# Two-layer deformable and whitening convolution: pieces of one channel half by 2048 pixels in the second pass, and twelve sixteenths of image 0 held in SBUF between its statistics and its convolution

## What is computed

```
x = x + deform_conv(group_norm(x))    # layer 0: statistics of every image, a convolution that gives
                                      # values v and sampling offsets, bilinear sampling of v, 1x1 out
x = x + zca_whiten(group_norm(x))     # layer 1: one 16-channel covariance over ALL images, its inverse
                                      # square root, then a 256x256 (block-diagonal) map of every pixel
```

## Time and profile before

| | us |
|---|---|
| median of 3 executions | 6123.9 |
| lowest, highest | 6122.75, 6130.23 |
| the profiled execution's own time | 6122.9 |
| its span in the trace | 6121.2 |
| busy VectorE, TensorE (matmul), GpSimd | 4902.5 (80%), 4252.8 (69%), 3889.7 (64%) |
| DRAM read, written | 1074.6 MB, 536.9 MB |

### The profile page before, as it was taken

How to read it: one execution, slowest core, us unless ns; L and a number is a source line. 1 busy time by engine, 2 the same in 40 slices (tenths; PEclk the granted TensorE clock), 3 DMA queues, 4 the chain that set the end, 5 groups by cost and what they waited for, 6 DMA issues and landing times.

```text
span 6121.2 us, 66619 instructions
## 1 busy us (share of the span) xinstructions
PE 4252.8 (69%) x16382; PEld 2641.4 (43%) x16382; DVE 4902.5 (80%) x12991; ACT 960.4 (16%) x2076; POOL 3889.7 (64%) x4115
## 2 busy tenths in 40 slices
PE   4867777777677767776777677767777554459776
PEld 2434444444444444444444444444444333344322
DVE  7888888888898889887988898888888666557554
ACT  1211111111111111111111111111111111100000
POOL 0077777777777777777777777777777777730000
PEclk9989988999899989888989899899888677779999
DMA  8978777888787878777887788877777554459999
GB/s 281 309 250 269 258 258 253 267 270 264 239 278 260 266 250 275 261 256 242 284 266 262 244 269 269 267 254 233 235 235 235 160 174 152 153 198 394 421 421 409
DMA packets 931609, 1612.85 MB, mean 263 GB/s; under 512 B 80944, under 2 KB 605872, under 8 KB 929456
## 3 DMA queue, kind: packets, MB, share of 16 engines
q0 software_dynamic: 196608, 537.13, 26.5%
q10 hardware_dynamic: 595968, 536.90, 25.8%
q1 hardware_dynamic: 138928, 537.74, 25.7%
HBM read 1074.58 MB, written 536.87 MB: 263 GB/s over the span
## 4 chain that ended last, share of the span: by engine, by line
POOL 59%; issue 21%; ACTq 6%; DVE 5%; DMA 4%; PE 3%; POOLq 0%; DVEq 0%; ACT 0%; SPq 0%
POOL patch L923 59%; ACTq L1314 6%; DMA out_dram<-patch 1%; DMA xs_mem<-x_dram 1%; DVE bst L438 1%; DVE patch L622 1%; DVE vring L505 1%; DMA v<-vring 1%; DMA patch<-x 0%; PE psA L1031 0%; DMA patch<-x_dram 0%; PE psO L1173 0%; PE psT L1173 0%; PE psA L1173 0%; DMA patch<-v,index_now 0%
## 5 line engine op out<-in xcount | busy, mean ns | idle before, releaser
L923 POOL DMA_INDIRECT patch<-v,index_now x4096 | 3883.8, 948 | 1530.7 <-issue 1528.8
L1031 PE MATMUL psA<-wB,xa_mem 128*128 128x364 f32 x3824 | 1525.4, 545 | 728.3 <-DVE taps L517 720.2
L622 DVE TENSOR_TENSOR patch<-patch,psI 128x384 f32<-128x384 f32 x2048 | 1038.0, 548 | 546.9 <-DMA patch<-v,index_now 516.4
L1031 PEld LDWEIGHTS psA<-wB,xa_mem 128*128 128x128 f32 x3824 | 787.1, 218 | 1339.7 <-DVE taps L517 919.4
L1063 PE MATMUL psO<-sampT,wO_sb 128*128 128x512 f32 x2048 | 973.5, 620 | 0.0
L1091 PE MATMUL psG<-x1T 128*128 128x129 f32 x4096 | 615.0, 313 | 434.3 <-DVE gram L658 433.4
L1091 PEld LDWEIGHTS psG<-x1T 128*128 128x128 f32 x4096 | 576.6, 225 | 461.7 <-issue 238.0
L1197 ACT ACTIVATE vring<-vring 128x512 f32<-128x512 f32 x512 | 320.2, 625 | 2413.9 <-DVE vring L505 2413.9
L1077 PE MATMUL psT<-ident,xr_mem 128*128 128x128 f32 x2048 | 312.5, 302 | 389.0 <-DVE xr_mem L649 388.4
L1063 PEld LDWEIGHTS psO<-sampT,wO_sb 128*128 128x128 f32 x2048 | 392.4, 202 | 400.2 <-issue 399.9
L1077 PEld LDWEIGHTS psT<-ident,xr_mem 128*128 128x128 f32 x2048 | 264.5, 158 | 506.3 <-issue 420.3
(11 more groups left out here) (213 smaller groups left out, 2941.0 us busy)
## 6 DMA issues: line engine op xcount, KB each, us to landing
v<-vring ACTq DMA_DIRECT2D x128, 2048.0 KB, 13.4
xa_mem<-x_dram SPq DMA_DIRECT2D x128, 1024.0 KB, 9.6
xr_mem<-x_dram SPq DMA_DIRECT2D x128, 1024.0 KB, 6.4
x<-xr_mem ACTq DMA_DIRECT2D x128, 1024.0 KB
xs_mem<-x_dram SPq DMA_DIRECT2D x112, 1024.0 KB, 6.6
patch<-v,index_now POOLq DMA_INDIRECT x4096, 3.8
patch<-x SPq DMA_DIRECT2D x64, 1024.0 KB, 14.2
out_dram<-patch ACTq DMA_DIRECT2D x64, 1024.0 KB, 32.5
```

Source lines behind the costliest of these rows:

```text
L622: eng.tensor_tensor(two, two, w4[:, 2 * v:2 * v + 2, 0:3].unsqueeze(3).to_broadcast([P, 2, 3, CG]), ALU.mult)
L923: eng.indirect_dma_start(out=patch[n][:, t, :], out_offset=None, in_=v2_flat[k], in_offset=bass.IndirectOffsetOnAxis(ap=index_now[n][:, t: ...
L1031: mm = eng.matmul(conv_bank[wide][r][:, 0:NA], xa[m][j][:, c, r * W:(r + 1) * W], wB[:, c, :], start=(c == 0), stop=(c == CC - 1))
```

## The change

It has three pieces.

**Second pass.** A piece is now one channel half by 2048 pixels: the same 1 MB, now 128 rows of 8 KB. Pieces 0 to 7 of an image are the lower half, 8 to 15 the upper. The number of pieces, matmuls, additions, loads and stores is unchanged.

**Statistics of image 0.** All 16 pair tiles have their own place in SBUF: pairs 12 to 15 ("passing", loaded and measured first) lie in the two `xa_mem`, `xs_mem` and `samp_mem`; pairs 0 to 7 in the four `patch` buffers (2 MB transfers); pairs 8 and 9 in `xr_mem`, pairs 10 and 11 in the two `xa_mem`, after the passing tiles there have been measured. Only those last two, and image 1's first tile in `xs_mem`, wait for VectorE.

**Convolution of image 0.** Pairs 0 to 11 (`HELD` = 12) are read by TensorE where they lie. Twelve loads of 1 MB go; pairs 12 to 15 are loaded again as before. For this first call SyncE's and TensorE's 16 pairs are written out instead of looped.

```diff
+HELD = 12
+AGAIN = tuple(range(HELD, PAIRS))
+YB = 4 * BP
+NY = CC * PIX // YB
...
+        held = [two[:, :, k * (2 * BP):(k + 1) * (2 * BP)] for two in held_two for k in range(2)]
+        held += [mem[:, :, :, :].rearrange("p c j n -> p c (j n)") for mem in (*xr_mem, *xa_mem)]
+        passing = [mem[:, :, :, :].rearrange("p c j n -> p c (j n)") for mem in (*xa_mem, xs_mem)]
...
+        y_half = [j // (PIX // YB) for j in range(NY)]
+        y_at = [j % (PIX // YB) * YB for j in range(NY)]
...
             def load_s(b, i):
+                if isinstance(b, int) and isinstance(i, int) and (b, i) == (1, 0):
+                    eng.wait_ge(st0_used, len(AGAIN))
...
             def load_a(b, i, m):
+                if stays(b, i):
+                    return
...
-                    with eng.Fori(0, PIX // S0 // 2) as i:
-                        for j in range(2):
-                            at = eng.snap((i * 2 + j) * S0)
-                            eng.wait_ge(st0_used[j], i + 1)
-                            alone(eng)
-                            eng.dma_start(xs0[j], x_v[s, :, :, bass.ds(at, S0)])\
-                               .then_inc(st0_ld[j], 16)
+                    for i in AGAIN:
+                        eng.dma_start(passing[i - HELD], x_v[s, :, :, i * (2 * BP):(i + 1) * (2 * BP)])\
+                           .then_inc(piece_ld[i], 16)
+                    for n in range(RING):
+                        eng.dma_start(held_two[n], x_v[s, :, :, n * (4 * BP):(n + 1) * (4 * BP)])\
+                           .then_inc(piece_ld[2 * n], 16)
+                    for i in range(2 * RING, HELD):
+                        if i >= HELD - 2:
+                            eng.wait_ge(st0_used, i - (HELD - 2) + 1)
+                            alone(eng)
+                        eng.dma_start(held[i], x_v[s, :, :, i * (2 * BP):(i + 1) * (2 * BP)])\
+                           .then_inc(piece_ld[i], 16)
...
-                eng.dma_start(y_buf[j], x1_v[0, :, :, j * YB:(j + 1) * YB]).then_inc(y_ld[j], 16)
+                eng.dma_start(y_buf[j], x1_v[0, :, y_half[j], y_at[j]:y_at[j] + YB]).then_inc(piece_ld[j], 16)
...
+                        row = held[i][:, c, (j * ROWS + r) * W:(j * ROWS + r + 1) * W] if stays(b, i) \
+                            else xa[m][j][:, c, r * W:(r + 1) * W]
```

More of the change, by code:

```diff
@@ L194, in deform_zca_kernel @@
         map_v = sem("map_v")
-        y_ld = [sem(f"y_ld{j}") for j in range(NY)]
+        piece_ld = [sem(f"piece_ld{j}") for j in range(NY)]
         y_mm = sem("y_mm")
@@ L226, in run, with pairs @@
             image(B - 2, B - 1, None, None)
-        def pairs(eng, pair):
+        def pairs(eng, pair, unrolled=False):
+            if unrolled:
+                for i in range(PAIRS):
+                    pair(i, i % 2, i // 2)
+                return
             for i in range(2):
@@ L309, in deform_zca_kernel @@
         cnow = area(biasB, CC * P, CC)
-        y_buf = [mem[:, :, :, :].rearrange("p c j n -> p c (j n)") for mem in (*xa_mem, xs_mem)]
+        y_buf = [mem[:, :, :, :].rearrange("p c j n -> p (c j n)") for mem in (*xa_mem, xs_mem)]
         y_buf += [v[:, half * ROWS:(half + 1) * ROWS, :, :, :].rearrange("p r g k e -> p (r g k e)")
[L312 to L315, removed]
+                  for v in vring for half in range(2)]
+        y_buf += [weight[:, :]]
+        y_buf += [area(p_n[:, :, :].rearrange("p j e -> p (j e)"), k * YB, YB)
+                  for p_n in patch for k in range(2)]
+        y_half = [j // (PIX // YB) for j in range(NY)]
+        y_at = [j % (PIX // YB) * YB for j in range(NY)]
         y_bank = ((*psO, *psA), (*psT, psI, psG))
@@ L391, in pair @@
                         load_r(g, i, m, q)
-                pairs(eng, pair)
+                pairs(eng, pair, g is None)
             def first_conv():
@@ L729, in image @@
                 if a is None and g is None:
[L730 to L737, removed]
-                                                       xs0[j][:, c, n * BP:(n + 1) * BP])
-                            ins.then_inc(st0_used[j], 1)
+                    for i in (*AGAIN, *range(HELD)):
+                        src = held[i] if i < HELD else passing[i - HELD]
+                        if not (i < 2 * RING and i % 2):
+                            eng.wait_ge(piece_ld[i], 16)
+                        for c in range(CC):
+                            for n in range(2):
+                                ins = eng.bn_stats(bst[:, c, i * 2 + n, :], src[:, c, n * BP:(n + 1) * BP])
+                        ins.then_inc(st0_used, 1)
                     return
@@ L1020, in conv_rows @@
             def conv_rows(b, i, m, q, j, rows, wide):
-                if j == 0 and 0 in rows:
-                    eng.wait_ge(xa_ld[m], (b * (PAIRS // 2) + q) * 16 + 16)
+                if j == 0 and 0 in rows and not stays(b, i):
+                    eng.wait_ge(xa_ld[m], xa_turn(b, q))
                 for r in rows:
```

51 lines of the change are left out of this document (26 added, 25 removed).

## The result

| | kernel before | changed kernel |
|---|---|---|
| median of 9 executions each, us | 6125.36 | 6110.16 |
| lowest, highest | 6121.14, 6130.43 | 6103.56, 6111.59 |
| ratio to before, 95% interval | | 0.9971 [0.9962, 0.9979] |
| the profiled execution's own time, span | 6122.9, 6121.2 | 6105.31, 6103.6 |
| DRAM read, MB | 1074.6 | 1062.0 |

The account below looks back on a forecast made before the run. The fetch block was taken as fixed, the second pass as bound by DMA bytes over rate, and the front as improvable. Gains of 9.9 + 2.3 + 8.8 + 1.0 + 12.5 = 34.5 us took 6122.9 to 6088.4 us, range 6072 to 6105.

Parts of the forecast that it names:

- the prediction's own sign: Reasons count as wrong if the front gains under 15 or over 28 us, or the second pass runs at ≤422 or 436 GB/s.
- 1. Statistics: Statistics of image 0, start to `prep`: loads end the stage at 51.4 us instead of 61.28, -9.9 us.
- 2. First period: Up to pair 2's first eviction: image 1's second statistics tile lands in 7.0 us instead of 9.28, -2.3 us.
- 3. The 13 pairs: Convolution of image 0: DMA stops binding, each pair falls from 12.76 to 12.08 us, VectorE's chain; -8.8 us.
- 4. The last v store: Image 0's last v store, before the first fetch: lands sooner than 14.86 us behind a shorter backlog, -1.0 us.
- 5. Second pass: Second pass: 8 KB rows raise the DMA rate from 421 to 430 GB/s, 597.8 to 585.3 us, -12.5 us.
- A: Rival: second pass stays at 421 GB/s, only the front gains, 22.0 us; 6101 us in all, chance 0.14.
- B: Rival: second pass reaches the ceiling of 437 GB/s, -21.9 us beside the front's -22.0; 6079 us, chance 0.12.
- E: Rival: second-pass stores in 8 KB rows lose rate, +53 us against the front's -22; 6154 us, chance 0.03.
- Rival C: Second pass gets half the gain, 425 GB/s, -5.7 us in that term; 6095 us, chance 0.16.
- rival D: Pairs stay at 12.76 us, last v store no sooner; only statistics, first period and half the second-pass gain: 6105 us, chance 0.05.

Follow-up runs that it names:

- half_pass: The changed kernel with its second pass ended after 4 of 8 images, the other four outputs left out; executed once, span 6922.5 us.
- rows_only: The kernel before with only the second pass changed to the new pieces with 8 KB rows; 7262.34 us, 0.9993 of the kernel before.
- v_first: The changed kernel with SyncE's loads after image 1's last statistics tile held until image 0's last v store landed; 6108.38 us, 0.9957 of the kernel before.
- after_again: The changed kernel unaltered, measured again on another chip; 7332.26 us, 0.9975 of the kernel before.

## Why the prediction was wrong

The direction and the separation into front and second pass held. Of the five places named, three gained less than forecast (the statistics, the 13 pairs, the second pass) and two gained nothing. By the prediction's own sign its reasons for the front were wrong: the first fetch came 10.5 us earlier, where less than 15 was to count as that and 22.0 was forecast.

*1. Statistics, -9.9 against -6.8.* The step that failed is the path. The sum let the loads end the stage ("Last byte at 48.5 us, 0.3 us to its wait, four `bn_stats`"), with VectorE alone 0.8 us shorter ("VectorE alone would need 50.5 us"). The last byte came near its forecast, at 49.0 us, but VectorE was 3.0 us behind it. Its own chain was the longer one: the first `bn_stats` at 12.06 us instead of 11.5, 64 of them at 0.61 us, and two stops, 2.49 us for the first 2 MB transfer and 0.68 us later, together 54.3 us of the 54.46. I had counted the landing of a double tile's bytes and not that nothing of it may be used before its end. With single tiles the stage is 1.15 us shorter and the loads are its bound again. (The "16 tiles in 9.78 us" of the prediction are 16 `bn_stats`, which is four pair tiles.)

*2. First period, -2.3 against +0.7.* The second statistics tile landed in 8.82 us, not 7.0. The step that failed is "it shares the engines with the first v store and with the load of pair 2's `xa_mem`. That load goes". In both kernels the tile moves no byte for the first 4.0 us, in which the v store, issued 4.4 us ahead of it, is all but finished; the load of `xa_mem` was issued behind the tile, and taking it away brought 0.46 us. Whether the tile's packets stood behind the store's in the engines or were formed late, the runs don't tell. One more thing stands in this stretch: the first eight matmuls of the convolution, 2.77 us in the chain before, take 3.93.

```profile
69.65 2.77 PE psA L1031 x8
```
```profile
62.81 3.93 PE psA L1058 x8
```

This 1.16 us is the difference of two executions and isn't shown to be the change's. In TensorE's timelines the same eight take 2.8 to 4.3 us in the 14 profiles of kernels whose TensorE pairs are written out (4.1 in the changed kernel, 2.8 in half_pass), and 3.0 and 3.2 us in before and rows_only. I had set written-out code at nothing, with about 1 us a pair as its worst case, for which I had no row; no later pair shows any such cost.

*3. The 13 pairs, -8.8 against -5.0.* The DMA did stop binding (share 0.86 to 0.90), and VectorE's chain did come next, as the forecast said. What failed is "I read 12.08 us as VectorE's own chain for a pair". The shortest pair of a loop of two is the one without the branch; the mean of both, 12.21, is the floor: 13 x 0.13 = 1.7 us. The rows had said so: VectorE's waits for transfers summed to 6.9 us, and the 1.9 us missing to 8.8 were called near. The other 2.2 us are the ends of the stage, by VectorE's first taps eviction of each pair: the first pair takes 13.1 us, the last two 12.7 and 12.8. "absorbed by two `vring` buffers" was wrong for the statistics tile, which has one buffer (two waits on the chain, for the tiles issued at 225.7 and 238.8 us; a third, for that of 91.04 us, lies in the first pair).

*4. The last v store, -1.0 against +0.6.* Its landing didn't shorten (15.42 us against 14.86), so the step that failed is "behind a backlog that is then shorter": what makes it late is the loads issued beside it, which are the same. v_first shows 8.7 us without them.

*5. Second pass, -12.5 against -6.2 (mean over profiles -7.9).* The mechanism held and the term was mis-sized. The rate is 427 and not 430 GB/s: 251.7 MB / 427 = 589.5 us, -8.3 instead of -12.5. The end, one engine alone for nearly 7 us where the rate faded out over 4 before, takes back time of the size of the remaining 2.1 us.

Of the rivals, A and B fell with 427, and so did E: stores in 8 KB rows lose nothing. Rival C's half, 425 GB/s, was nearly right on the second pass, and rival D's half on the front ("the front does not pay"): the kernel did both at once, which no case of mine held. That D's 6105 is the profiled execution's own time is luck: D counted -9.9, -2.3, 0, 0 and -6.25 where -6.8, +0.7, -5.0, +0.6 and -6.2 were measured. D had 0.05 because I asked whether the statistics tile would be late in every pair; among the 13 it is late in the first and in the last ones only, which costs 2 of the 11.5 us by which the front fell short.

## What to carry to other kernels

When a stage passes from one bound to the next, the floor is the mean of the new bound's period over one whole turn of its loop, branches included, and not the shortest period seen. When several engines stand within 5% of each other, subtract from a forecast what each handover between stages costs: a single buffer or a transfer released as a whole keeps the old wait alive at the ends of a stage even where its middle is free. Before a landing is shortened by what is taken away beside it, see in the view by queue which transfer moves while it waits. A rate for a new row length is best taken from two known row lengths and a cost per row, rather than from the fastest slices of a view; here a run with 2 KB rows could have given it before the change.

## What was not expected of the hardware

A register and branch step of VectorE's loop costs 0.42 us every second pair, and writing the loop out saved 0.54 us a pair, although none of it counts as busy. A 1 MB load issued 4.4 us behind a 2 MB store in 512-byte rows moved nothing for its first 4.0 us, in both kernels. At the end of a long pass at full DMA rate most engines stand for 4 to 7 us while one to a few work on; after half a pass this was shorter in the one execution of each kind. And chips differ by more than any of these edits: on three of the five used, the 4096 fetches take 6.2 to 6.3 ms instead of 5.13 or 5.14, and the last fetch to the first map up to 20 us more, with a granted clock of 0.80 to 0.81 instead of 0.88 to 0.89 over the span; in after_again GpSimd waits 994 us for its indices, where it waited 1.8 us in before. The runs don't tell what that comes from.
